# Graph network, edge counts: the weighted keys of the fixed tiles move from VectorE to GpSimd

## The reference

```
agg = x + segment_sum(x[src], tgt, n)                 # first layer, both directions, twice
cnt = segment_sum(ones, dst * 8 + edge_type, n * 8)   # last layer, twice
agg = segment_sum(msg / clip(cnt, 1), dst, n)
```

## Time and profile before

| | us |
|---|---|
| three runs | 5125.5, 5124.34, 5118.6 (median 5124.34) |
| the profiled execution, its own time | 5122.0 |
| its span in the trace | 5120.2 |
| VectorE busy over the span | 3000.6 |
| TensorE matmuls busy over the span | 3898.8 |
| GpSimd busy over the span | 886.3 |

### The profile page before, as it was taken

The page is one execution under the profiler, slowest core; times in us unless marked ns, Lnnn a source line. Parts: engine busy times, 40 slices in busy tenths (PEclk is TensorE's granted clock), DMA queues, the critical chain, the costliest instruction groups (busy, mean ns, idle before and its releaser), DMA issues. The chain is left out here.

```text
span 5120.2 us, 111920 instructions
## 1 busy us (share of the span) xinstructions
PE 3898.8 (76%) x33516; PEld 2678.1 (52%) x33731; DVE 3000.6 (59%) x6855; ACT 1928.4 (38%) x2458; POOL 886.3 (17%) x994
## 2 busy tenths in 40 slices
PE   2666667674677777776588888788888699979997
PEld 1222227673334434343344444444444599979997
DVE  6988886656333333333356555365555677767776
ACT  0111113300111111111265555455555565646664
POOL 1000000000677777776100000000000000000000
PEclk6888888896788899898599999799999899989998
DMA  2000007593566666665111111111111011111110
GB/s 100 32 32 32 32 32 267 215 248 101 126 145 144 145 144 145 145 144 117 37 65 51 52 63 51 40 52 61 54 51 64 28 45 38 45 34 39 45 38 26
DMA packets 385754, 425.73 MB, mean 83 GB/s; under 512 B 269055, under 2 KB 334710, under 8 KB 384390
## 3 DMA queue, kind: packets, MB, share of 16 engines
q1 hardware_dynamic: 221430, 277.46, 17.7%
q0 software_dynamic: 44480, 97.87, 8.1%
q10 hardware_dynamic: 119760, 49.33, 3.4%
HBM read 317.96 MB, written 106.12 MB: 83 GB/s over the span
## 5 line engine op out<-in xcount | busy, mean ns | idle before, releaser
L1648 POOL DMA_INDIRECT er_got<-edge_q_parts,er_now x880 | 833.6, 947 | 275.7 <-issue 259.5
L1795 DVE TENSOR_TENSOR_SCAN er_run<-er_cut,er_carry,er_out 64x512 f32 x220 | 279.8, 1272 | 444.6 <-PE er_back L1697 419.7
L750 PE MATMUL code_ps<-code_hot_l,code_hot_k 128*128 128x400 bf16 x1600 | 355.1, 363 | 222.4 <-DVE code_hot_l L721 216.6
L2692 PE MATMUL r1d_up<-r1d_xs,r1d_dig 128*128 128x193 bf16 x5000 | 435.8, 247 | 14.8 <-DVE r1d_dig L2630 14.8
L2692 PE MATMUL r0d_up<-r0d_xs,r0d_dig 128*128 128x193 bf16 x5000 | 435.6, 247 | 14.9 <-DVE r0d_dig L2630 14.9
L2692 PEld LDWEIGHTS r1d_up<-r1d_xs,r1d_dig 128*128 128x128 bf16 x5000 | 429.1, 98 | 15.7 <-issue 15.1
L2692 PEld LDWEIGHTS r0d_up<-r0d_xs,r0d_dig 128*128 128x128 bf16 x5000 | 428.9, 98 | 15.8 <-issue 15.2
L1679 PE MATMUL er_pre<-identb,er_got 128*128 128x128 bf16 x2640 | 357.4, 240 | 65.7 <-ACTq L1761 53.7
L1679 PEld LDWEIGHTS er_pre<-identb,er_got 128*128 (+1 forms) x2640 | 255.2, 104 | 238.7 <-issue 156.2
L750 PEld LDWEIGHTS code_ps<-code_hot_l,code_hot_k 128*128 128x128 bf16 x1600 | 149.2, 105 | 418.9 <-DVE code_hot_l L721 307.4
L2579 ACT ACTIVATE r1d_dig<-r1d_raw 128x3200 bf16<-128x3200 uint16 x100 | 281.4, 2862 | 199.9 <-DVE r1d_raw L2624 199.9
(11 more groups left out here) (402 smaller groups left out, 6437.4 us busy)
## 6 DMA issues: line engine op xcount, KB each, us to landing
er_line<-target_line SPq DMA_DIRECT2D x220, 128.0 KB
edge_runs<-er_rows ACTq DMA_DIRECT2D x220, 128.0 KB
pair_codes<-code_codes SPq DMA_DIRECT2D x25, 800.0 KB, 3.3
c0s_code<-pair_codes SPq DMA_DIRECT2D x25, 800.0 KB, 8.0
count_panels<-c0s_panel SPq DMA_DIRECT2D x25, 800.0 KB, 5.3
count_rows<-c0s_rows ACTq DMA_DIRECT2D x25, 800.0 KB, 6.3
c1s_cols<-count_panels SPq DMA_DIRECT2D x25, 800.0 KB, 5.9
c1s_rows<-count_rows SPq DMA_DIRECT2D x25, 800.0 KB, 7.3
```

The costliest lines, as they stand in the source:

```text
L750: last = pe.matmul(ps[u][:, c * CUT:c * CUT + HALF], keys, lows[:, c * HALF:(c + 1) * HALF], start=fresh, stop=True, skip_group_check=True)
L1648: pool.indirect_dma_start(out=got[:, i, j, :], out_offset=None, in_=k.q_parts[:, :], in_offset=bass.IndirectOffsetOnAxis(ap=now[:, i * G + ...
L1795: v.tensor_tensor_scan(run[:, :], cut[:, ds((g + (CUTS - back_)) % CUTS, 1), :] .rearrange("p a e -> p (a e)"), out[:, ds((g + back_) % 2, ...
L2692: last = pe.matmul(up[:, b, t * DST:(t + 1) * DST], dig[r][:, c, :], xs[:, c, 0:DST], start=(c == 0), stop=(c == W - 1), skip_group_check= ...
```

## The change

GpSimd gets a loop over all windows that makes the weighted keys of the eight fixed tiles, with the same operation and operands as VectorE's. Before each window it waits for `laid`, before each step for `used`, each as an instruction by itself (`wait_alone`: a wait and an increment of a semaphore that nobody waits for). Behind a step's two keys it counts up `keyed`. VectorE makes only the wide columns of the fixed tiles, and still both arrays of the further tiles. TensorE waits for `hots` and for `keyed` before a step's matmuls. GpSimd's wait for the ten stores moves behind the loop.

```diff
+        keyed, passed = sem("keyed"), [sem(f"passed{e}") for e in range(2)]
...
             for n in range((MOST - SURE) * G // SPARE):
                 pool.dma_start(spares[n], spare[:, :]).then_inc(filled, 16)
+            pool.wait_ge(iotas, 4)
+            with pool.Fori(0, WC - SETS + 1, SETS) as w:
+                for u in range(SETS):
+                    wait_alone(pool, laid, w + u + 1, passed[0])
+                    for s in range(STEPS):
+                        wait_alone(pool, used, w * STEPS + (u * STEPS + s + 1), passed[0])
+                        for j in (2 * s, 2 * s + 1):
+                            last = pool.tensor_scalar(hot_k[:, j, :], iota_k[:, :], key_of[u][:, j, 0:1],
+                                                      key_of[u][:, j, 1:2], ALU.is_equal, ALU.mult)
+                        last.then_inc(keyed, 1)
             pool.wait_ge(filled, 16 * ((MOST - SURE) * G // SPARE))
...
             def fixed(w, u, s):
                 v.wait_ge(used, w * STEPS + (u * STEPS + s + 1))
                 for j in (2 * s, 2 * s + 1):
-                    v.tensor_scalar(hot_k[:, j, :], iota_k[:, :], key_of[u][:, j, 0:1], key_of[u][:, j, 1:2],
-                                    ALU.is_equal, ALU.mult)
                     last = v.tensor_scalar(hot_l[:, j, :], iota_l[:, :], low_of[u][:, j, 0:1], None, ALU.is_equal)
                 last.then_inc(hots, 1)
...
             def fixed(w, u, s):
                 pe.wait_ge(hots, w * STEPS + (u * STEPS + s + 1))
+                pe.wait_ge(keyed, w * STEPS + (u * STEPS + s + 1))
```

## The result

The changed kernel takes 5256.8 us (median of 4 runs, 5252.5 to 5257.8) against 5122.6 for the kernel before (median of 4): a ratio of 1.0259, interval 1.0244 to 1.0274. It is slower by 134 us, where 80 us of gain were forecast.

The account below looks back on a forecast made before the run. VectorE was taken to bound the count stage. Blocks falling from 25.78 to 22.6 us, 25 times, gain 80 us: 5122.0 less 80 is 5042, plus 2.3 for the median gives 5044 us; range 5012 to 5200.

Parts of the forecast that it names:

- 800 keys arrive on GpSimd: Count stage: a weighted key on GpSimd was priced at 0.41 us, with bounds of 0.23 and 0.84.
- rival A: GpSimd's key is dear, so the kernel is slower: 5194 us at a 0.60 us key, 5339 at 0.84; chance 0.21.
- What bounds the kernel now: Count stage: VectorE sets the pace, 0.56 us a fixed tile, 25.78 us a block of four windows, 25 blocks 644 us.
- floor of 21.7 us: TensorE's time for a block with operands always there: 5.56 idle, 5.4 at the lower clock, 10.8 for the other matmuls.
- The break-even: Block of 24t + 10.6 us, t being a fixed tile's time by turns, equals 25.78 at t = 0.63, key 0.48 us.
- The turns: VectorE and GpSimd partly exclude each other: wide column holds 0.24 us, key 0.26, so a fixed tile takes 0.50, not 0.56.
- rival B: VectorE and GpSimd each hold the other off for a whole instruction: block 30.5 us, time 5242 us; chance 0.10.
- Waits and queues: GpSimd's 20 lone waits a block and gaps behind keys, and TensorE's second wait: taken as 0, with 20 us kept possible.
- (1): Sign in the changed kernel's profile: TensorE's restarts 21.7 to 24.5 us apart, not 25.78.
- (2): Sign: wide columns of 0.45 to 0.55 us in the mean, not 0.42, and GpSimd's keys as long, waits included.
- (3): Sign: TensorE's idle time ahead of a fixed step put down to GpSimd's key about as often as to the wide column.
- (4): Sign: all stages after the count stage stay as before.

Follow-up runs that it names:

- e8: The kernel before, with GpSimd running six operations twice into an unread array while VectorE reads its table and runs nothing: 5122.1 us in a single run.
- e7: The kernel before, with ScalarE instead of VectorE making the key of every second fixed tile, in two operations; no keys on GpSimd: 5070.8 us, ratio 0.9902.
- e9: As e7, with the arrays `hot_k` and `hot_l` holding 16 fixed tiles in place of 8: 5074.6 us, ratio 0.9903.
- e5: The changed kernel, with VectorE's wide columns of the fixed tiles reading their row of numbers as 25 rows of 32 with gaps: 5197.3 us, ratio 1.0143.
- e3: The kernel before, VectorE making everything; GpSimd makes every second key again into an array nobody reads, and TensorE waits for it: 5135.3 us, ratio 1.0027.
- e2: The changed kernel, with GpSimd making only the keys of odd fixed tiles and VectorE those of even ones: 5114.2 us, ratio 0.9981.

## Why the prediction was wrong

**The step that failed** is "800 keys arrive on GpSimd": "I take the copy and two scalars, 0.293 + 0.12 = 0.41 us, as the copy is the nearest row that reads a tile and writes one." The key has 0.79 us of its own (e8). The copy (0.29) and the scalars (0.14, against 0.12) were sized rightly; a compare and a multiply add 0.36, and the sum had nothing for them. The 60 ns that stood for a scalar are also not a scalar's alone: L736 adds and compares, L721 only compares, so they hold a second operation too. The select of 282 ns in the earlier trace rows, which I held against rival A because it compares too, says nothing on a compare in this operation.

**What bounds the kernel now** held in the main: VectorE set the pace, and each key taken off it frees 0.22 us (in e7 wide columns without a key between them start 0.34 us apart). The 217 us put down to the wide column were less of a sign than I took them for: 165 are restarts and the stage's first wait. TensorE's restart is 5.3 to 5.7 us in every variant, and its floor of 21.7 us agrees with e9, where the same terms make 21.5 (5.3 + 5.6 + 10.6). e7 shows that the relief is worth having.

**The break-even** was named: rival A, with a chance of 0.21, put it at a key of 0.48 us alone, and the mechanism that won is A, a GpSimd that is busy through the whole stage. Its size was off the other way. With 0.79 its formula gives t = 0.94, a block of 33.2 us and 5308; measured 31.3 and 5257. The formula has VectorE lose as much by a turn as GpSimd. In truth a key loses 0.16 us in the mean and VectorE's wide column 0.02.

**The turns** exist only in part. They were read from four iotas, where each side waited for the other's end. In the stage five of VectorE's operations run, whole or in part, beside one key of 1.34 us, so neither holds the other off for a whole instruction, and rival B is out. The Trainium skill (SBUF — State Buffer, Who interferes with whom) says that the two contend when VectorE runs in a two-port mode, and that the second comer is then blocked for the whole of the first's instruction. The first half agrees with e5, where no key beside the wide columns with gaps takes over 0.80 us; the second does not agree with the 0.444 us of the wide column in the changed kernel. How the two share in detail stays open: 400 keys of GpSimd's cost VectorE's key 9 ns in the mean in e3 and 38 in e2, where it has fewer operations to run.

**Waits and queues** cost nothing on GpSimd, as taken: its keys with nothing beside them follow each other at 0.773 us from start to start, less than one lasts, and no slower across a lone wait than within a step. TensorE's second wait was not measured by itself; e7 has one too, and is faster. What the sum lacked is a wait of GpSimd's: at a block's start it fills the arrays and then stands still until TensorE has restarted, 33 us in all and 73 in e5.

**The forms to watch for**: (1) restarts 31.3 us apart, wrong; (2) wide columns at 0.444, just under the stretch named, keys at 0.95, wrong; (3) TensorE's idle time put down to the key nearly alone (308 of 349 us; the column's 36.5 are one wait at the stage's start), not as often to the column, wrong; (4) later stages unchanged, right. The closing condition, keys over 0.63 us apart and a stage that is GpSimd's, is what came.

## What to carry to other kernels

Price an operation on another engine by a row of the same operation there; a copy on GpSimd tells nothing of a compare and multiply. Where no row has it, time it alone in a gap of the kernel, as e8 did for a few microseconds. Before work is moved to an idle engine, ask which engine it disturbs by running at all: half of the keys gave 9 us on GpSimd and 52 us on ScalarE, though ScalarE needs two operations for each.

## What the runs showed of the hardware that was not expected

- GpSimd's compare and multiply of 128 bf16 columns by two scalars from memory takes 0.79 us, of 64 columns 0.58: by these two widths an estimated 3.3 ns a column and 0.37 us fixed. VectorE's whole operation takes 0.309. The Trainium skill (GPSIMD Engine Reference, Performance versus the Vector engine) gives 1.03 cycles an element for a body of up to two operations, and reckons with 1.2 GHz; the slope between the two widths would be about four such cycles, an estimate.
- An input with gaps between its rows takes VectorE's wide column from 0.422 to 0.618 us, and GpSimd's keys beside it take 0.79 us, as alone (e5).
- VectorE and GpSimd do not lose alike: beside VectorE's full stream a key goes from 0.79 to 1.18 us, VectorE's key from 309 to 318 ns (e3). With half of VectorE's keys gone it is 1.16 us and 347 ns (e2).
